# Places of the edges in source order: two column halves, one product for both halves of the base, six PSUM banks

## The chip, the cores and the metric

The kernel runs on one core of a Trainium2 chip. The metric is the device time of one execution in microseconds. The kernel before was run three times; its median is 3303.43 us.

## The reference, cut to what matters

The reference is a graph network of four blocks over 3125 nodes and 53125 edges, each edge with a source `src` and a target `dst` (sorted by `dst`) and 128 edge features. What matters here is the start, and the third block, a GIN with batch norm over the edges:

```python
for l in range(3):
    x = jnp.concatenate([h[src], e], axis=1)      # per edge
    x = x @ W1[l].T + b1[l]
    mu, var = jnp.mean(x, axis=0), jnp.var(x, axis=0)
    x = relu((x - mu) * rsqrt(var + BN_EPS) * gamma[l] + beta[l])
    h = jax.ops.segment_sum(x @ W2[l].T + b2[l], dst, num_segments=n_nodes)
    if l < 2:
        h, e = relu(h), relu(e)
```

The batch statistics need sums of `relu(e)` over the edges of each source node. Edges come sorted by target, so the kernel also writes the edge rows into DRAM a second time, ordered by the 128-node tile of their source (`by_tile`). For that each edge needs its place in this order, which is an integer worked out in the kernel: the number of edges of all lower tiles, plus those of its own tile in earlier chunks of 128 edges, plus those of its own tile in lower partitions of its own chunk.

## The kernel before, in words

Nodes lie in 25 tiles of 128 (`N_TILES`), edges in 104 groups of 4 chunks (`NG * GC` = 416 chunks), edge 128 c + p at partition p of column c. Every engine has a program of its own, written out by hand, and semaphores order them; nothing is scheduled by a planner.

The stages that matter, by the spans of the profile:

- **Setup, 0 to 37 us.** VectorE (DVE) makes `masks[:, t, :]`, for each of the 25 source tiles the 128x416 one-hot of the edges whose source is in tile t (L1277). TensorE (PE) counts them per chunk (L772), DVE scans the counts into `chunk_base`, a 25x416 table of where each chunk's edges of each tile begin, and splits it into two bf16 terms `base_hi` and `base_lo` (L1288, L1289).
- **Places, 37 to 70 us.** For each tile t PE accumulates three 128x416 products in one PSUM bank: the strictly upper triangle times the mask (L783, the number of earlier edges of that tile in the chunk), and a broadcast column of the identity times `base_hi` (L784) and times `base_lo` (L785). DVE copies the result where the mask is set (L1294, `copy_predicated`), alternately into two accumulators. Four banks are used in turn. At the end one addition of the two accumulators writes the integers `place` (L1296).
- **Counting, 70 to 350 us.** DVE, only after L1296, makes one-hots of the edges of each group (L1307) and adds the PE's products into a dense adjacency matrix in SBUF (L1318), 104 groups. PE multiplies them (L817) and, from group 21 on, does part of the first aggregation beside it (L793, L802).
- **Block 0, 350 to 546 us**: dense aggregations and two MLPs, ending in the tables `tabs` and `tabd`, one row for each node, in SBUF `tN`.
- **Block 1, from 568 us**: a pass over all edges. GpSimd (POOL) gathers rows of `tabs` from DRAM (L503); the other engines follow group by group.

Beside these, **POOL** writes the edge rows to `by_tile` with indirect DMAs (L2267, two for a pair of chunks, `put_rows`), from the moment `place` exists: pairs 0 to 127, then 128 to 187, then it goes on to block 1's gathers; the last 20 pairs follow after these. **SyncE's queue (SP)** loads the rows of each pair into a ring of four stages (`load_pairs`, L2396) and can load pair q only when pair q - 4 has been written. In SP's program the loads of pairs up to 187 stand ahead of the stores of `tabs` and `tabd` to DRAM (L2444), and POOL waits for all eight of these stores before the first gather of block 1.

```python
            put_rows(*PUT_ENDS[0:2])          # POOL; PUT_ENDS = (0, 128, 188, 208)
            ...
            load_pairs(PUT_ENDS[1] + SPILLS * STAGES, PUT_ENDS[2])    # SP: pairs 148 to 187
            ...
            for n in (1, 3, 5, 6):            # SP: stores of the tables
```

Of the kernel before, what the change touches and what calls it, by code (L numbers as in the profile page):

```python
# [51 lines left out]
PAIRS = NG * GC // 2  # L52
PUT_ENDS = (0, 128, 188, PAIRS)

# [121 lines left out]
def build(nc, x_n, x_t, e_t, e_rows, src_g, idx_g, dst_p, dst_row, src_p, weights, cols, rows, eps, gammas, out):  # L176
    with ExitStack() as ctx:
        def sb(name, shape, dt=F32):
            return ctx.enter_context(nc.sbuf_tensor(name, shape, dt))
# [9 lines left out]
        ident_h = sb("ident_h", [D, D], BF16)  # L189
# [38 lines left out]
        upper_h = sb("upper_h", [D, D], BF16)  # L228
        tile_sel = sb("tile_sel", [D, 2 * N_TILES - 1], BF16)
        tile_col = sb("tile_col", [D, 4])  # L230
# [98 lines left out]
        base_hi, base_lo = (scratch[0:N_TILES, 2048 + k * NG * GC // 2:2048 + (k + 1) * NG * GC // 2].bitcast(BF16) for k in range(2))  # L329
# [421 lines left out]
        def pe_program(pe):  # L751
# [16 lines left out]
            pe.wait_ge(S["consts"], 10)  # L768
            for t in range(N_TILES):
                if t in (0, MASKS_FIRST):  # L770
                    pe.wait_ge(S["setup_to_pe"], 5 if t else 4)
                mm = pe.matmul(cnt_ps, tile_sel[:, N_TILES - 1 - t:2 * N_TILES - 1 - t], masks[:, t, :], start=(t == 0),  # L772
                               stop=(t == N_TILES - 1))
            mm.then_inc(S["setup_to_dve"], 1)
            pe.wait_ge(S["setup_to_pe"], 6)
# [3 lines left out]
            for t in range(N_TILES):  # L779
                if t > 3:  # L780
                    pe.wait_ge(S["setup_to_pe"], 8 + t - 4)
                to, tile = psum[:, t % 4, 0:NG * GC], ident_h[0:N_TILES, t:t + 1].to_broadcast([N_TILES, D])
                pe.matmul(to, upper_h[:, :], masks[:, t, :], start=True, stop=False)  # L783
                pe.matmul(to, tile, base_hi, start=False, stop=False)  # L784
                pe.matmul(to, tile, base_lo, start=False, stop=True).then_inc(S["setup_to_dve"], 1)  # L785
# [88 lines left out]
            pe.wait_ge(S["setup_to_pe"], 33)  # L874
# [32 lines left out]
            def gin(wa, wb, fold=False):  # L907
                pe_product(pe, T.turns("a" * N_BLOCKS), [(W(wa), a0)], ("gin_in", T["gin_in"]))
                if fold:
                    pe.transpose(st_ps[:, 0:D], W("msg_2"), ident[:, :])  # L910
                    pe.transpose(st_ps[:, D:2 * D], row("msg_b2"), ident[:, :]).then_inc(S["setup_to_dve"], 1)
                if fold:
                    pe.wait_ge(S["setup_to_pe"], 35)
                    pe.matmul(st_ps[:, 2 * D:3 * D], diag[:, :], W("upd_a"), start=True, stop=True)
                    pe.matmul(st_ps[:, 3 * D:3 * D + 1], W("upd_a"), msg_col, start=True, stop=True).then_inc(S["fold_mm"], 1)
                else:
                    pe_product(pe, T.turns("a" * N_BLOCKS), [(W(wb), a0)], blocks_of=("gin_hid", T["gin_hid"]))
                    count_gin(T)
# [64 lines left out]
            pe.wait_ge(S["setup_to_pe"], 36)  # L983
            pe.matmul(x_ps[0:N_TILES, 0:2], upper[0:N_TILES, 0:N_TILES], tile_col[0:N_TILES, 0:2], start=True, stop=True
                      ).then_inc(S["setup_to_dve"], 1)
            pe.wait_ge(S["setup_to_pe"], 37)
# [196 lines left out]
        def dve_program(dve):  # L1183
# [87 lines left out]
            v.did(dve.tensor_copy(upper_h[:, :], upper[:, :]))  # L1271
            for to in place_by:
                v.did(dve.memset(to, 0.0))
# [16 lines left out]
            for t in range(N_TILES):  # L1290
                dve.wait_ge(S["setup_to_dve"], 6 + t)
                if t > 1:
                    dve.wait_ge(S["setup_to_pe"], 8 + t - 2)
                dve.copy_predicated(place_by[t % 2], masks[:, t, :].bitcast(U16), psum[:, t % 4, 0:NG * GC]).then_inc(S["setup_to_pe"], 1)  # L1294
            dve.wait_ge(S["setup_to_pe"], 7 + N_TILES)
            dve.tensor_tensor(place[:, :], place_by[0], place_by[1], ALU.add).then_inc(S["tile_tables"], 1)  # L1296
            dve.wait_ge(S["tile_tables"], 1)
# [49 lines left out]
            dve.wait_ge(S["setup_to_dve"], 31)  # L1347
# [222 lines left out]
            dve.wait_ge(S["setup_to_dve"], 32)  # L1570
# [58 lines left out]
            dve.wait_ge(S["setup_to_dve"], 33)  # L1629
# [14 lines left out]
            dve.wait_ge(S["setup_to_dve"], 34)  # L1644
# [204 lines left out]
        def act_program(act):  # L1849
# [260 lines left out]
            def two_passes(l):  # L2110
# [29 lines left out]
                act.wait_ge(S["tile_tables"], 2)  # L2140
# [99 lines left out]
        def pool_program(pool):  # L2240
# [21 lines left out]
            def put_rows(lo, hi):  # L2262
                for q in range(lo, hi):
                    k = q % STAGES
                    pool.wait_ge(S[f"from_dram{k}"], 16 * (q // STAGES + 1))
                    for c in range(2):
                        pool.indirect_dma_start(by_tile[:, :], bass.IndirectOffsetOnAxis(ap=place[:, 2 * q + c:2 * q + c + 1], axis=0),  # L2267
                                                stage[:, k, c, :], None).then_inc(S[f"put{k}"], 16)

            put_rows(*PUT_ENDS[0:2])  # L2270
# [107 lines left out]
        def sp_program(sp):  # L2378
# [122 lines left out]
            for l in range(N_LAYERS2):  # L2501
# [9 lines left out]
                sp.wait_ge(S["tile_tables"], 2)  # L2511
# [120 lines left out]
```

## Time and profile before

| what | value |
|---|---|
| three runs | 3301.45, 3303.43, 3308.19 us |
| span of the profiled execution | 3301.0 us |
| PE busy | 2649.1 us (80%) |
| DVE busy | 1984.1 us (60%) |
| ACT busy | 1271.9 us (39%) |
| POOL busy | 2154.0 us (65%) |
| mean granted TensorE clock | 0.894 |

The span runs from the first to the last instruction of the profiled execution; the time of a run holds what lies around it as well. The profile gives the span of its own execution alone, so the two are told apart here only by the median: 3303.43 less 3301.0 is 2.4 us. In the profile times are us from the start of the span; PEld is the load of a weight tile, PE the matmul; `L1294` is a line of the kernel before.

### The profile page before, as it was taken

How to read it: one execution, taken by the hardware profiler on the slowest of the kernel's cores; microseconds unless marked ns; L12 is line 12 of the kernel's file. 1: busy time of each engine (PE TensorE's matmuls, PEld its weight loads, DVE VectorE, ACT ScalarE, POOL GpSimd, SP SyncE). 2: the span in 40 equal slices, each digit the busy share in tenths (PEclk: the TensorE clock that was granted, in tenths of full speed). 3: DMA queues.
4: the chain of work that ended last, by engine and by line, in shares of the span. 5: the costliest groups of instructions: out<-in, count | busy, mean ns of one | idle time of the engine just before them, and what ended most of it. 6: DMA issues, size and time to landing. Idle time of an engine off the chain costs nothing. (4 is left out here: it accounts for less than half of the span.)

```text
span 3301.0 us, 59411 instructions
## 1 busy us (share of the span) xinstructions
PE 2649.1 (80%) x14001; PEld 1764.8 (53%) x14001; DVE 1984.1 (60%) x3553; ACT 1271.9 (39%) x3069; POOL 2154.0 (65%) x2211
## 2 busy tenths in 40 slices
PE   5689895777767878888889998667779877677998
PEld 1234443556656557777766656445556555454444
DVE  6999694544444467777779847555554655555111
ACT  4777514333333456666667622111112211112111
POOL 1777776777777767777758747777755777774000
PEclk7799998777677899999989999999989999998999
DMA  2343455755665389999949745555534555555000
GB/s 98 104 108 107 150 183 151 207 165 166 165 170 161 106 295 317 331 321 321 325 156 327 277 135 171 153 158 154 158 103 149 170 156 156 157 156 179 23 1 20
DMA packets 305072, 570.42 MB, mean 173 GB/s; under 512 B 54465, under 2 KB 140406, under 8 KB 303510
## 3 DMA queue, kind: packets, MB, share of 16 engines
q1 hardware_dynamic: 204582, 299.39, 29.3%
q0 software_dynamic: 86528, 219.09, 22.4%
q10 hardware_dynamic: 13824, 50.34, 3.8%
q8 instruction: 57, 0.93, 0.1%
q14 instruction: 81, 0.66, 0.1%
HBM read 465.21 MB, written 103.66 MB: 172 GB/s over the span
## 5 line engine op out<-in xcount | busy, mean ns | idle before, releaser
L503 POOL DMA_INDIRECT region<-tab,region x624 | 602.7, 966 | 285.4 <-issue 202.4
L1037 PE MATMUL psum<-w_all,region 128*128 128x256 f32 x2496 | 642.6, 403 | 0.7 <-ACT region L2143 0.7
L2267 POOL DMA_INDIRECT by_tile<-stage,place x416 | 408.4, 982 | 197.5 <-issue 126.7
L1037 PEld LDWEIGHTS psum<-w_all,region 128*128 128x128 f32 x2496 | 489.2, 203 | 68.2 <-issue 2.1
L587 ACT COPY region<-psum 128x256 f32<-128x256 f32 (+1 forms) x420 | 143.1, 341 | 852.6 <-PE psum L580 852.6
L580 PE MATMUL psum<-region 128*64 128x256 f32 (+1 forms) x1664 | 222.0, 391 | 193.9 <-DVE region L1797 119.5
L503 POOL DMA_INDIRECT tN<-tab,region x312 | 300.1, 962 | 95.1 <-issue 94.2
L503 POOL DMA_INDIRECT tA<-tab,region x312 | 297.8, 954 | 95.1 <-issue 94.4
L1048 PE MATMUL psum<-region 128*128 128x256 f32 x1040 | 277.1, 414 | 79.8 <-DVE region L1677 79.5
L594 PEld LDWEIGHTS psum<-fold,region 128*128 128x128 f32 x1470 | 215.1, 206 | 152.6 <-issue 152.6
L594 PE MATMUL psum<-fold,region 128*128 128x64 f32 x1470 | 276.4, 309 | 0.0
L1048 PEld LDWEIGHTS psum<-region 128*128 128x128 f32 x1040 | 204.6, 204 | 132.5 <-issue 103.4
L580 PEld LDWEIGHTS psum<-region 128*64 128x64 f32 x1664 | 114.3, 149 | 266.9 <-issue 176.4
L503 POOL DMA_INDIRECT region<-tabs,region x208 | 205.4, 988 | 72.7 <-issue 71.4
L503 POOL DMA_INDIRECT tN<-tabs,region x208 | 203.7, 979 | 63.4 <-issue 59.4
L1792 DVE TENSOR_TENSOR psum<-region,psum 128x1024 f32<-128x1024 f32 x104 | 127.8, 1229 | 192.6 <-DMA region<-tab,region 178.7
L580 PE MATMUL psum<-tN,region 128*64 128x256 f32 (+1 forms) x1040 | 135.4, 382 | 108.1 <-DVE region L527 50.1
L839 PE MATMUL psum<-region,acc 128*128 128x512 fp8e4 (+1 forms) x1050 | 208.7, 363 | 14.4 <-ACT acc L1940 10.3
L2135 ACT ACTIVATE region<-region,part 128x128 f32<-128x128 f32 x524 | 166.1, 387 | 68.2 <-PE psum L1048 61.7
L1792 DVE TENSOR_TENSOR psum<-tA,psum 128x1024 f32<-128x1024 f32 x78 | 95.9, 1229 | 146.0 <-DMA tA<-tab,region 129.3
L996 PE MATMUL psum<-w_all,region 128*128 128x128 f32 x832 | 174.4, 377 | 0.0
L2368 POOL TENSOR_TENSOR region<-node_no,dst_rel 128x256 f32<-128x256 f32 x104 | 133.4, 1283 | 58.3 <-ACT region L2177 46.2
(403 smaller groups left out, 4658.9 us busy)
## 6 DMA issues: line engine op xcount, KB each, us to landing
region<-e_t SPq DMA_DIRECT2D x416, 256.0 KB
region<-by_tile SPq DMA_DIRECT2D x131, 264.0 KB, 3.0
stage<-e_rows SPq DMA_DIRECT2D x208, 132.0 KB
pre_dram<-region ACTq DMA_DIRECT2D x48, 512.0 KB, 6.0
pre_dram<-tN ACTq DMA_DIRECT2D x48, 512.0 KB, 6.0
region<-pre_dram SPq DMA_DIRECT2D x48, 512.0 KB
tN<-pre_dram SPq DMA_DIRECT2D x48, 512.0 KB, 5.1
tA<-dst_row SPq DMA_DIRECT2D x78, 256.0 KB
```

Of the source, the lines that this page charges most:

```text
L503: pool.indirect_dma_start(ring[j][:, c, at:at + width], None, table[:, :], bass.IndirectOffsetOnAxis(ap=idx[:, c:c + 1], axis=0)).then_inc ...
L580: mm = pe.matmul(acc_ps[at:at + WIN, j % 2, 0:halves * D], oh_ring[:, j % OH_SLOTS, c, :], ring[j][:, c, 0:halves * D], start=(c < 2), sto ...
L587: act.copy(win_ring[:, slot, 0:halves * D], acc_ps[:, slot, 0:halves * D]).then_inc(S["win_out"], 1)
L594: mm = pe.matmul(turned(slot)[:, h * WIN:(h + 1) * WIN], win_ring[:, slot, h * D:(h + 1) * D], fold[:, :], start=True, stop=True)
L839: mm = pe.matmul(psum[:, b, 0:hi - lo], parts[p][:, t, :], adj[:, t, lo:hi], start=(p == 0 and t == 0), stop=(p == 2 and t == N_TILES - 1))
L996: pe.matmul(part, e_ring[:, j % E_SLOTS, edges], W("msg_e"), start=(c == 0), stop=False, skip_group_check=True)
L1037: mm = pe.matmul(banks[:, 2 * (j % 2) + c // 2, (c % 2) * 256:(c % 2) * 256 + 256], e_ring[:, j % E_SLOTS, c * D:(c + 1) * D], W(f"ee{l}") ...
L1048: mm = pe.matmul(unit_ps(m), u_both[:, m % 2, c, D:2 * D], u_both[:, m % 2, c, :], start=(c == 0), stop=(c == GC - 1))
L1792: dve.tensor_tensor(edge_ps(j), p, edge_ps(j), ALU.add).then_inc(S["pre"], 1)
L2135: r = act.activation(u_both[:, m % 2, c, D:2 * D], u_rows[:, m % U_ROWS, c, 0:D], ACT.Relu, scale=unit_mask[:, bass.ds(u * GC + c, 1)])
L2267: pool.indirect_dma_start(by_tile[:, :], bass.IndirectOffsetOnAxis(ap=place[:, 2 * q + c:2 * q + c + 1], axis=0), stage[:, k, c, :], None) ...
L2368: pool.tensor_tensor(off_ring[:, j % 2, :].rearrange("p (c n) -> p c n", c=GC), node_no[:, 0:WIN].unsqueeze(1).to_broadcast([D, GC, WIN]), ...
```

## The change

The places are worked out in two halves of 208 columns, all 25 tiles of the left half first, then all of the right (`n` = 0 to 49). The two base terms lie in one 64-row operand (hi at rows 0 to 24, lo at rows 32 to 56, zeros between), and a column of `tile_both`, which is set at rows t and 32 + t, takes both in one product. The bank ring has six places, three triangle products are issued ahead (the first three before the bases exist), and `place` is written in two halves, each with an increment of `tile_tables`. POOL starts its writes after the first and waits for the second before pair 104. All later counts of the setup semaphores are moved up by 25.

```diff
+PLACE_HALVES = (slice(0, NG * GC // 2), slice(NG * GC // 2, NG * GC))
+PLACE_SLOTS, TRIANGLES_AHEAD = 6, 3
+TOTALS_SET, BASES_SET = 5, 7
...
+            def triangle(n):
+                half, t = divmod(n, N_TILES)
+                if n >= PLACE_SLOTS:
+                    pe.wait_ge(S["setup_to_pe"], BASES_SET + n - PLACE_SLOTS + 1)
+                pe.matmul(psum[:, n % PLACE_SLOTS, 0:NG * GC // 2], upper_h[:, :], masks[:, t, PLACE_HALVES[half]],
+                          start=True, stop=False)
...
+            for n in range(TRIANGLES_AHEAD):
+                triangle(n)
...
-            for t in range(N_TILES):
-                if t > 3:
-                    pe.wait_ge(S["setup_to_pe"], 8 + t - 4)
-                to, tile = psum[:, t % 4, 0:NG * GC], ident_h[0:N_TILES, t:t + 1].to_broadcast([N_TILES, D])
-                pe.matmul(to, upper_h[:, :], masks[:, t, :], start=True, stop=False)
-                pe.matmul(to, tile, base_hi, start=False, stop=False)
-                pe.matmul(to, tile, base_lo, start=False, stop=True).then_inc(S["setup_to_dve"], 1)
+            for n in range(2 * N_TILES):
+                half, t = divmod(n, N_TILES)
+                pe.matmul(psum[:, n % PLACE_SLOTS, 0:NG * GC // 2], tile_both[0:WIN, t:t + 1].to_broadcast([WIN, D]),
+                          base_both[:, PLACE_HALVES[half]], start=False, stop=True).then_inc(S["setup_to_dve"], 1)
+                if n + TRIANGLES_AHEAD < 2 * N_TILES:
+                    triangle(n + TRIANGLES_AHEAD)
...
+            v.did(dve.tensor_tensor(tile_both[:, :], ident_h[:, 0:N_TILES], ident_h[:, 32:32 + N_TILES], ALU.add))
+            v.did(dve.memset(base_both, 0.0))
...
-            for t in range(N_TILES):
-                dve.wait_ge(S["setup_to_dve"], 6 + t)
-                if t > 1:
-                    dve.wait_ge(S["setup_to_pe"], 8 + t - 2)
-                dve.copy_predicated(place_by[t % 2], masks[:, t, :].bitcast(U16), psum[:, t % 4, 0:NG * GC]).then_inc(S["setup_to_pe"], 1)
-            dve.wait_ge(S["setup_to_pe"], 7 + N_TILES)
-            dve.tensor_tensor(place[:, :], place_by[0], place_by[1], ALU.add).then_inc(S["tile_tables"], 1)
-            dve.wait_ge(S["tile_tables"], 1)
+            for half, part in enumerate(PLACE_HALVES):
+                for t in range(N_TILES):
+                    n = half * N_TILES + t
+                    dve.wait_ge(S["setup_to_dve"], TOTALS_SET + n + 1)
+                    if n > 1:
+                        dve.wait_ge(S["setup_to_pe"], BASES_SET + n - 1)
+                    dve.copy_predicated(place_by[n % 2][:, part], masks[:, t, part].bitcast(U16),
+                                        psum[:, n % PLACE_SLOTS, 0:NG * GC // 2]).then_inc(S["setup_to_pe"], 1)
+                dve.wait_ge(S["setup_to_pe"], BASES_SET + (half + 1) * N_TILES)
+                dve.tensor_tensor(place[:, part], place_by[0][:, part], place_by[1][:, part], ALU.add).then_inc(S["tile_tables"], 1)
+            dve.wait_ge(S["tile_tables"], 2)
...
-            put_rows(*PUT_ENDS[0:2])
+            put_rows(0, PAIRS // 2)
+            pool.wait_ge(S["tile_tables"], 2)
+            put_rows(PAIRS // 2, PUT_ENDS[1])
```

The order on PE at the start of the places, before (`upper_h` is the triangle, `acc` holds the masks, `tN` the bases, `tile_sel` selects a row of the counts):

```order
L772 MATMUL psum<-acc,tile_sel 25x416 x25
L776 MATMUL psum<-tile_col,upper 25x1
L783 MATMUL psum<-acc,upper_h 128x416
L784 MATMUL psum<-tN,ident_h 128x416
L785 MATMUL psum<-tN,ident_h 128x416
L783 MATMUL psum<-acc,upper_h 128x416
L784 MATMUL psum<-tN,ident_h 128x416
L785 MATMUL psum<-tN,ident_h 128x416
```

and the same place in the changed kernel, where L778 is the triangle and L795 the product of both base terms:

```order
L784 MATMUL psum<-acc,tile_sel 25x416 x25
L778 MATMUL psum<-acc,upper_h 128x208 x3
L790 MATMUL psum<-tile_col,upper 25x1
L795 MATMUL psum<-tN,tile_both 128x208
L778 MATMUL psum<-acc,upper_h 128x208
L795 MATMUL psum<-tN,tile_both 128x208
L778 MATMUL psum<-acc,upper_h 128x208
L795 MATMUL psum<-tN,tile_both 128x208
```

Three triangles have moved ahead of the small product with `tile_col`. After that PE changes between a 64-row and a 128-row weight tile at every instruction, where before two of three in a row had 25 rows.

The order on DVE at the end of the places, before:

```order
L1294 COPY_PREDICATED tN<-acc,psum 128x416
L1294 COPY_PREDICATED acc<-acc,psum 128x416
L1296 TENSOR_TENSOR place<-acc,tN 128x416
L1307 TENSOR_SCALAR tN<-tN 128x500 x8
```

and in the changed kernel at the end of the first half (L1311 is the copy, L1314 the addition into `place`):

```order
L1311 COPY_PREDICATED tN<-acc,psum 128x208
L1311 COPY_PREDICATED acc<-acc,psum 128x208
L1314 TENSOR_TENSOR place<-acc,tN 128x208
L1311 COPY_PREDICATED tN<-acc,psum 128x208
L1311 COPY_PREDICATED acc<-acc,psum 128x208
```

The first addition, on which POOL's first write now waits, stands ahead of the second 25 copies; the one-hots of the counting (L1325 there) still stand behind all 50.

## Rows read from the trace of the kernel before

**Rows 1.** Page, part 4: the chain that ended last.

```profile
PE 3%; DVE 0%; ACT 0%; issue 0%; DVEq 0%; ACTq 0%
```

**Rows 2.** Waits (engine, line, what for: us in total, times, longest), POOL and SP.

```profile
POOL by_tile L2267 <- DVE place L1296: 67.2, 1, 67.2
SPq L2403 <- DMA by_tile<-stage,place: 401.7, 174, 56.4
```

**Rows 3.** Timeline (start us, us, engine, line, op), around the hand-over to block 1.

```profile
540.42 10.08 SPq L2396 DMA_DIRECT2D stage<-e_rows  x5
544.32 0.89 DVE L1532 TENSOR_TENSOR tN<-psum,row_all 128x512 f32<-128x512 f32 x2 [1.21 <-PE psum L690]
551.22 0.38 SPq L2444 DMA_DIRECT2D tabs<-tN  x1
556.45 3.70 SPq L2444 DMA_DIRECT2D tabs<-tN  x1
557.67 0.96 POOL L2267 DMA_INDIRECT by_tile<-stage,place  x1 [0.30 <-issue]
568.21 0.98 POOL L503 DMA_INDIRECT region<-tabs,region  x1 [9.58 <-issue]
572.30 0.69 DVE L1589 TENSOR_TENSOR region<-tA,win_node 128x512 bf16<-128x512 int32 x1 [26.22 <-DMA region<-tabd]
```

**Rows 4.** Timeline, end of the places.

```profile
67.64 0.55 PE L785 MATMUL psum<-tN,ident_h 25*128 25x416 bf16 x1
68.23 0.62 DVE L1294 COPY_PREDICATED acc<-acc,psum 128x416 f32<-128x416 uint16 x1 [0.64 <-PE psum L785]
68.88 0.59 DVE L1296 TENSOR_TENSOR place<-acc,tN 128x416 int32<-128x416 f32 x1
69.51 2.16 DVE L1307 TENSOR_SCALAR tN<-tN 128x500 bf16<-128x500 f16 x8
70.41 1.39 POOL L2267 DMA_INDIRECT by_tile<-stage,place  x1 [67.15 <-DVE place L1296]
```

**Rows 5.** Timeline, start of the places; one tile of 25.

```profile
37.02 0.35 PE L783 MATMUL psum<-acc,upper_h 128*128 128x416 bf16 x1 [1.89 <-DVE tN L1289]
39.14 0.53 PE L783 MATMUL psum<-acc,upper_h 128*128 128x416 bf16 x1
39.60 0.52 PE L784 MATMUL psum<-tN,ident_h 25*128 25x416 bf16 x1
39.92 0.55 PE L785 MATMUL psum<-tN,ident_h 25*128 25x416 bf16 x1
40.40 0.53 PE L783 MATMUL psum<-acc,upper_h 128*128 128x416 bf16 x1
```

**Rows 6.** Windows (stretch: length, busy PE, PEld, DVE, ACT, POOL, PEclk, DMA share, GB/s).

```profile
39.00:68.00 29.00, 29.00 (x70) 5.23 (x69) 14.24 (x23) 0.00 (x0) 0.00 (x0) 0.50 0.00 1
83.00:100.00 17.00, 8.90 (x20) 2.31 (x20) 15.11 (x31) 10.67 (x29) 13.11 (x13) 0.50 0.37 99
```

**Rows 7.** Groups by shape on DVE, 0 to 70 us (busy us, mean ns).

```profile
L1256 DVE TENSOR_TENSOR tN<-tN,psum 128x208 f32<-128x208 f32 x2 | 0.7, 350 | 0.0
L1273 DVE MEMSET acc<- 128x416 f32 x1 | 0.4, 405 | 0.0
```

**Rows 8.** Timeline, PE, block 1: groups of four with 128-row and 64-row weights.

```profile
598.84 0.39 PE L1000 MATMUL psum<-region 128*128 128x128 bf16 x4
599.16 0.39 PE L1003 MATMUL psum<-region 64*128 64x128 bf16 x4
599.48 0.66 PE L580 MATMUL psum<-region 128*64 128x128 f32 x8
```

**Rows 9.** Timeline, PE, counting, where part of the aggregation begins beside it.

```profile
133.88 1.82 PE L817 MATMUL psum<-tN 128*128 128x500 bf16 x4 [1.52 <-DVE tN L1307]
137.32 1.01 PE L817 MATMUL psum<-tN 128*128 128x500 bf16 x4
138.17 1.46 PE L802 MATMUL psum<-region,acc 128*128 128x512 fp8e4 x6
```

More of the change, by code:

```diff
@@ L229, in build @@
         tile_sel = sb("tile_sel", [D, 2 * N_TILES - 1], BF16)
+        tile_both = sb("tile_both", [D, N_TILES], BF16)
         tile_col = sb("tile_col", [D, 4])
@@ L328, in build @@
         chunk_base = scratch[0:N_TILES, 2560:2560 + NG * GC]
-        base_hi, base_lo = (scratch[0:N_TILES, 2048 + k * NG * GC // 2:2048 + (k + 1) * NG * GC // 2].bitcast(BF16) for k in range(2))
+        base_both = scratch[0:WIN, 2048:2048 + NG * GC // 2].bitcast(BF16)
+        base_hi, base_lo = base_both[0:N_TILES, :], base_both[32:32 + N_TILES, :]
         part2_w = part2[:, :, :].rearrange("p t f -> p (t f)").bitcast(F32)
@@ L873, in pe_program @@
             pe.transpose(x_ps[:, D:2 * D], row("ln_g"), ident[:, :])
-            pe.wait_ge(S["setup_to_pe"], 33)
+            pe.wait_ge(S["setup_to_pe"], 58)
             pe.matmul(x_ps[:, 0:1], ones[:, :], small[:, 14:15], start=True, stop=True).then_inc(S["setup_to_dve"], 1)
@@ L912, in gin @@
                 if fold:
-                    pe.wait_ge(S["setup_to_pe"], 35)
+                    pe.wait_ge(S["setup_to_pe"], 60)
                     pe.matmul(st_ps[:, 2 * D:3 * D], diag[:, :], W("upd_a"), start=True, stop=True)
@@ L982, in pe_program @@
             pe.wait_ge(S["pass_ready"], T["pass_ready"] + 1)
-            pe.wait_ge(S["setup_to_pe"], 36)
+            pe.wait_ge(S["setup_to_pe"], 61)
             pe.matmul(x_ps[0:N_TILES, 0:2], upper[0:N_TILES, 0:N_TILES], tile_col[0:N_TILES, 0:2], start=True, stop=True
                       ).then_inc(S["setup_to_dve"], 1)
-            pe.wait_ge(S["setup_to_pe"], 37)
+            pe.wait_ge(S["setup_to_pe"], 62)
             pe.matmul(x_ps[:, 0:3 * TABLE], ones[0:N_TILES, :], unit_all, start=True, stop=True).then_inc(S["setup_to_dve"], 1)
@@ L1346, in dve_program @@
             dve.tensor_scalar(small[:, 14:15], small[:, 14:15], NP - 0.5, None, ALU.is_lt).then_inc(S["setup_to_pe"], 1)
-            dve.wait_ge(S["setup_to_dve"], 31)
+            dve.wait_ge(S["setup_to_dve"], 56)
             dve.tensor_tensor(irregular[:, :], x_ps[0:1, 0:1], small[0:1, 12:13], ALU.add).then_inc(S["irregular_set"], 1)
@@ L1568, in dve_program @@
             gin(1, tA, "g2", "bt2")
-            dve.wait_ge(S["setup_to_dve"], 32)
+            dve.wait_ge(S["setup_to_dve"], 57)
             dve.tensor_copy(diag[:, :], st_ps[:, 0:D]).then_inc(S["setup_to_pe"], 1)
@@ L1628, in dve_program @@
             dve.tensor_copy(units, whole).then_inc(S["setup_to_pe"], 1)
-            dve.wait_ge(S["setup_to_dve"], 33)
+            dve.wait_ge(S["setup_to_dve"], 58)
             dve.wait_ge(v.sem, v.did(dve.tensor_copy(tile_col[tiles_, 2:4], x_ps[tiles_, 0:2])))
@@ L1643, in dve_program @@
                                      op0=ALU.subtract, op1=ALU.mult).then_inc(S["setup_to_pe"], 1)
-            dve.wait_ge(S["setup_to_dve"], 34)
+            dve.wait_ge(S["setup_to_dve"], 59)
             v.did(dve.tensor_copy(unit_i, x_ps[0:1, 0:2 * TABLE]))
@@ L2139, in two_passes @@
                 relu_e(0, 0)
-                act.wait_ge(S["tile_tables"], 2)
+                act.wait_ge(S["tile_tables"], 3)
                 unit_relu(0, 0, 0)
@@ L2510, in sp_program @@
                 sp_table(sp, T.turns("adadadadadada") if l else table_turns, tab2, 2 * D)
-                sp.wait_ge(S["tile_tables"], 2)
+                sp.wait_ge(S["tile_tables"], 3)
                 sp.wait_ge(S["idx_all"], 32)
```

## The prediction

> **What bounds the kernel now.** The chain of waits comes first and says little: it follows only the end of the program, 3% of the span [rows 1]. So I read the waits next. Two stand out for this change: POOL waits 67.2 us, once, for the addition that writes `place`, and SP's queue waits 401.7 us in 174 pieces for POOL's writes to `by_tile` [rows 2]. The timeline then tells who is last where block 1 begins [rows 3]. DVE makes the last piece of the tables at 544.32 and is done with it 0.89 later, at 545.2. SP is still loading edge rows until 550.5, one load for each pair that POOL has written, and can issue the first table store only at 551.22. POOL's last write is at 557.67 and its first gather at 568.21, after the stores have landed; DVE then has sat idle for 26.22 us. So DVE and PE have 6 us in hand there, and what sets the start of block 1 is the row of POOL's writes, which starts at 70.41 when `place` exists [rows 4]. What comes after 568 follows from this start.
>
> That makes two chains from the places stage, and the change moves them by different amounts. **Chain Y**: first half of `place`, POOL's 376 writes, SP's loads, the eight stores, block 1. **Chain X**: both halves, the counting, block 0, the tables. I work out both shifts, and then which one block 1 sees.
>
> **The cost of one step of the places.** Before, a tile takes 1.26 us (39.14 to 40.40), and PE is busy without a gap (29.00 of 29.00 us) at the lower of its two levels, 1.2 GHz (granted clock 0.50) [rows 5, 6]. DVE's copy takes 0.62 and DVE waits 0.64 before each [rows 4]. So PE is the bound. Streaming 416 columns at 1.2 GHz is 0.347 us, three times 1.04; the other 0.22 is a weight load that is not hidden. The intervals say where: 0.46 after the triangle and 0.48 before the next one, but 0.32 between the two 25-row products [rows 5]. Block 1 shows the same for the new pair of shapes: four 128-column products in 0.32 us (598.84 to 599.16, then to 599.48), where streaming at 2.4 GHz is 0.213, so 0.11 more for each change between 128-row and 64-row weights [rows 8].
>
> In the changed kernel a step of 208 columns is one triangle and one base product, and both change the weight rows: 2 x 0.173 + 0.22 = 0.57 us at the lower level. The bounds: not below the DVE, whose copy of 208 columns I put at 0.38 (0.62 less the 0.24 by which an addition falls from 0.59 at 416 to 0.35 at 208 columns; between 0.35 and 0.62) plus 0.04 to the next, so 0.42; not above 0.46 + 0.48 = 0.94, the whole old intervals [rows 4, 5, 7]. I take 0.57, because two rows at either level agree on the 0.11.
>
> The Trainium skill ("TensorE: Matmul & The Clock Gate", on LDWEIGHTS) says that the engine pulls the next weight load ahead of a running matmul when row groups don't conflict or it goes to the background buffer. By that, with all loads hidden, a step would be 0.35 on PE and 0.42 on DVE. This trace shows it hidden only between equal row counts. The same page says that keeping TensorE busy without gaps brings it to the full clock; in the 29 us here it stayed at 0.50. Both rules would give the rival of the fast step below, and I give them little weight for that reason.
>
> **Part by part.**
>
> - *Added before the masks*: the sum `tile_both` (128x25) and the zero fill (64x416 bf16). Each is smaller than the 128x416 fill of 0.405 us [rows 7], so together 0 to 0.81; I take 0.35. It delays the bases by as much: the first base product starts at 37.02 + 0.35 = 37.37 [rows 5].
> - *Three triangles ahead*: they run while DVE makes the bases, in which PE sat idle 1.89 us just before 37.02 [rows 5]. The scan of the counts on DVE takes its time anyway, and the small product with `tile_col` is not needed before it. I cost them at nothing; if that cover were gone, 3 x 0.48 = 1.4 us.
> - *Six banks*: PE waited for no copy before (it was the bound), so nothing.
> - *Chain Y*: the 25th base product starts 24 x 0.57 later, at 51.0. Its copy starts 0.42 after (before it was 0.59 for twice the columns: 67.64 to 68.23), takes 0.38, then 0.04, the half addition 0.35, and POOL needs the 0.94 that lay between the end of the old addition (69.47) and its first write [rows 4]. That is 53.1, against 70.41: **Y = 17.3 us**. POOL's second wait, before pair 104, is 208 writes later. The 376 writes ran from 70.41 to 557.67, 1.30 us each [rows 3, 4]; POOL's one long wait in it is the first [rows 2], so it moves as a whole.
> - *Chain X*: 47 steps of 0.57, then two base products without a triangle between (0.17 each): the last starts at 64.4. With 0.42, 0.38, 0.04, 0.35 and 0.04 the one-hots start at 65.6 instead of 69.51: **X = 3.9 us**. Bounds from the step: +9.9 at 0.42, and -14 at 0.94.
> - *What block 1 sees*: SP's first store could go at 551.22 - 17.3 = 533.9. The burst from there to the first gather took 17.0 us before, which gives 550.9. But now the tables are not all ready: the last is there at 545.2 - 3.9 = 541.3, 7.4 after the burst starts, while before the store of the last full piece was issued 5.2 after (556.45). From 556.45 to the first gather were 11.8 us, part of it a backlog of the earlier stores [rows 3]; the whole of it behind 541.3 would be 553.1, none of the backlog gives 550.9. I take 551.5, near the lower end, since the first stores of the burst are still landing then. The gain is 568.2 - 551.5 = **16.7 us**.
> - *The semaphore counts moved by 25* cost nothing.
>
> Against its own time, the profiled span would go from 3301.0 to 3284.3. The median of the runs is 2.4 above the span, and I carry that: 3303.4 - 16.7 = 3286.7 us.
>
> **The rivals.**
>
> *Fast step.* The loads hide, or the granted clock stays at 1.00, and DVE is the bound at 0.42 us. For it: half of PE's stream now has 128-row weights, where it was a third, so the engine's work is another one than that which stayed at 0.50. Against it: rows 5, 6 and 8. The first half is done at 49.6 with POOL's start, so Y = 20.8 and X = 9.9; the tables are there at 535.3, and the burst ends at 568.2 - 20.8 = 547.4. Time: 3282.6.
>
> *Only chain X counts.* POOL's earlier start is eaten before 551, by stops in its row of writes or because the stores wait for something else, and block 1 moves with DVE and PE: 3303.4 - 3.9 = 3299.5. For it: the writes share the DMA engines with the adjacency's spill to DRAM, and both move. Against it: SP's 401.7 us of waits for these writes, and the 26.22 us that DVE is idle [rows 2, 3].
>
> *Halved columns do not halve the step.* At 0.94 us a step, Y is 8.2 and X is -14.1; the tables come at 559.3, and with some 7 us for the last stores without a backlog the gather starts at 566.3. Time: about 3301.5, no change. Against it: rows 8, where 128 columns take 0.08.
>
> *Slower: the counting loses its clock.* With 6 aggregation products beside a group, PE needs 137.32 to 139.46, 2.1 us at the upper level, under DVE's 2.5 a group; at the lower level it would need 1.82 + 6 x 0.427 = 4.4 [rows 9], which is 1.9 us more than DVE. Before, the level rose within a group or two of the start of this work, after it had been low with PE half busy from 83 to 100 [rows 6, 9]. The changed stage ends at another time, and if the level rose late, each group would cost 1.9 us on chain X. It cancels the gain from the ninth group on (X below -13), and at 14 groups the time is about 3311. Nothing speaks for it but that the level is not set by the program.
>
> **How the numbers follow.** The forecast has a chance of 0.63, with its own range of 3284 to 3290 (step 0.5 to 0.7). The fast step has 0.17, a partial give-back between forecast and chain X 0.06, chain X alone or the unhalved step 0.10, slower 0.04. From 3279 to 3297 holds the first three. A measurement of this kernel can tell 0.2% (6.6 us) from no change, so faster means below 3296.8: 0.63 + 0.17 + 0.06 = 0.86, less 0.01 for a partial give-back that goes beyond it; same 0.11; slower 0.04.
>
> **What would show it.** In the profile after: steps of 0.57 us on PE in the places with the granted clock at 0.50 (0.42 and DVE without waits would be the fast step); POOL's first write at 53; the first one-hot at 65.6; the first table store at about 534 and the first gather at 551 to 553, with DVE's idle time before it still over 20 us. The prediction is wrong if the gather moves by less than POOL's first write does by more than 3 us, or if anything after block 1 gives the gain back.

## The result and the profile after

Against six runs of the kernel before (three new ones beside the three of the prediction; median 3305.44 us, 3298.27 to 3311.43), six of the changed kernel give a median of 3284.8 us (3281.03 to 3286.75): ratio 0.9936, 95% interval 0.9925 to 0.9947. The change is faster by 0.64%. The forecast was 3286.7 us within 3279 to 3297. The profiled span went from 3301.0 to 3279.8 us, 21.2 less; the mean granted clock is 0.895 (0.894 before). The profiled execution of the changed kernel is its fastest (3281.03 us). Below, each profile shows one execution.

**One step of the places.** Timeline of the kernel after on PE, then on DVE (start us, us, engine, line, operation, count, idle time before it and what released it; L778 is the triangle, L795 the product of both base terms, L1311 the copy):

```profile
38.18 0.26 PE L795 MATMUL psum<-tN,tile_both 64*128 64x208 bf16 x1 [1.88 <-DVE tN L1304]
38.38 0.26 PE L778 MATMUL psum<-acc,upper_h 128*128 128x208 bf16 x1
38.57 0.26 PE L795 MATMUL psum<-tN,tile_both 64*128 64x208 bf16 x1
...
40.61 0.36 PE L778 MATMUL psum<-acc,upper_h 128*128 128x208 bf16 x1
40.90 0.35 PE L795 MATMUL psum<-tN,tile_both 64*128 64x208 bf16 x1
41.19 0.36 PE L778 MATMUL psum<-acc,upper_h 128*128 128x208 bf16 x1
```

```profile
38.48 0.39 DVE L1311 COPY_PREDICATED acc<-acc,psum 128x208 f32<-128x208 uint16 x1 [0.35 <-PE psum L795]
...
40.72 0.39 DVE L1311 COPY_PREDICATED tN<-acc,psum 128x208 f32<-128x208 uint16 x1 [0.18 <-PE psum L795]
```

From 40.61 to 41.19 PE issues a triangle and a base product: 0.58 us, and over the 19 steps from the copy at 40.72 to that at 51.61 the mean is 0.573, where it was 1.26 for twice the columns [rows 5]. DVE waits 0.18 before each copy, so PE still is the bound. Timeline on PEld:

```profile
40.90 0.10 PEld L795 LDWEIGHTS psum<-tN,tile_both 64*128 64x128 bf16 x1 [0.18 <-issue]
```

The load of the weights starts at 40.90, with its own product and not during the one before. In the kernel before, the load of the second 25-row product (40.87, 0.01 after the load of the first) stands 0.31 ahead of its product (41.18), behind a weight tile of its own row count; the next 128-row load waits for its own product at 41.66.

The first steps are faster, 0.39, at the higher granted clock. Windows of the kernel after (stretch: length, busy PE, PEld, DVE, ACT, POOL, granted clock, DMA share, GB/s), to be read beside [rows 6]:

```profile
37.00:40.00 3.00, 1.82 (x9) 0.85 (x9) 2.58 (x7) 0.00 (x0) 0.00 (x0) 0.94 0.00 0
40.00:66.00 26.00, 25.11 (x89) 9.08 (x88) 18.17 (x49) 0.00 (x0) 9.79 (x10) 0.50 0.14 40
```

**The end of the two halves.** Timeline on DVE and on POOL, which answer to [rows 4]:

```profile
52.03 0.38 DVE L1314 TENSOR_TENSOR place<-acc,tN 128x208 int32<-128x208 f32 x1
...
65.37 0.38 DVE L1311 COPY_PREDICATED tN<-acc,psum 128x208 f32<-128x208 uint16 x1
65.78 0.38 DVE L1314 TENSOR_TENSOR place<-acc,tN 128x208 int32<-128x208 f32 x1
66.20 2.55 DVE L1325 TENSOR_SCALAR tN<-tN 128x500 bf16<-128x500 f16 x8
```

```profile
53.34 1.15 POOL L2285 DMA_INDIRECT by_tile<-stage,place  x1 [50.09 <-DVE place L1314]
```

POOL starts 17.1 us earlier (70.41 to 53.34), the counting 3.3 us earlier (69.51 to 66.20).

**The hand-over to block 1.** Timeline of the kernel after on SP's queue, POOL and DVE, which answer to [rows 3]:

```profile
533.39 0.38 SPq L2464 DMA_DIRECT2D tabs<-tN  x1
...
538.63 3.82 SPq L2464 DMA_DIRECT2D tabs<-tN  x1
```

```profile
539.55 0.96 POOL L2285 DMA_INDIRECT by_tile<-stage,place  x1 [0.30 <-issue]
550.41 0.98 POOL L508 DMA_INDIRECT region<-tabs,region  x1 [9.90 <-issue]
```

```profile
538.83 0.89 DVE L1550 TENSOR_TENSOR tN<-psum,row_all 128x512 f32<-128x512 f32 x2 [1.20 <-PE psum L695]
...
553.90 0.69 DVE L1607 TENSOR_TENSOR region<-tA,win_node 128x512 bf16<-128x512 int32 x1 [13.31 <-DMA region<-tabd]
```

The first table store stands 17.8 us earlier (551.22 to 533.39) and so does the first gather (568.21 to 550.41). The tables are ready only 5.5 us earlier (544.32 to 538.83 for their last piece), so DVE's idle time before block 1 halves, from 26.22 to 13.31. From the hand-over to the end the lead of matching DVE instructions over those of before goes 18.4 us (at 573), 15.7 (1150), 12.1 (1700), 14.9 (2400), 18.7 (3041), 21.2 (3301). The last 2.7 us of it arise in the last dense pass of TensorE, whose first 108 us have a granted clock of 0.98 in the profile before and 1.00 in that after. Another 3.3 us arise earlier (15.4 at 3028, 18.7 at 3045), where the granted clock is 0.50 from 3028 to 3038 in the profile before and 1.00 in the same place (3012 to 3020) of that after. Nothing in the change touches either place, and I put both rises down to the clock of these two executions. Without them this pair of profiles would end some 15 us apart, less than the 17.8 of block 1; the medians lie 20.6 us apart, and what makes up the difference stays open.

### The profile page after: what moved, and what is told of

It reads as the page before. It is cut to its first block and busy times, and to the rows that moved or that the text cites. A ratio compares the mean times of both kernels' runs of the same rounds, so it can differ in the third digit from the quotient of the medians.

```text
span 3279.8 us, 59515 instructions
## 1 busy us (share of the span) xinstructions
PE 2644.0 (81%) x14026; PEld 1768.6 (54%) x14026; DVE 1990.8 (61%) x3581; ACT 1272.0 (39%) x3069; POOL 2157.4 (66%) x2211
## 3 DMA queue, kind: packets, MB, share of 16 engines
q1 hardware_dynamic: 204582, 299.39, 29.8%
## 5 line engine op out<-in xcount | busy, mean ns | idle before, releaser
L852 PE MATMUL psum<-region,acc 128*128 128x512 fp8e4 (+1 forms) x1050 | 205.5, 359 | 10.5 <-ACT acc L1958 7.5
```

Source lines behind the costliest of these rows:

```text
L852: mm = pe.matmul(psum[:, b, 0:hi - lo], parts[p][:, t, :], adj[:, t, lo:hi], start=(p == 0 and t == 0), stop=(p == 2 and t == N_TILES - 1))
```

## The experiments

Three questions: does the row of POOL's writes set the start of block 1, or the tables; what does each part of the change give; and what are the 0.11 us of a weight load that is not hidden. Unless another kernel is named, an edit is made to the changed kernel.

### e1 to e4: four kernels on a slow chip

One set ran on a chip on which the kernel before itself takes 4269.75 us (35 runs, 4241.92 to 4293.63). What they were to show:

```diff
e1_late_pool:  -            pool.wait_ge(S["tile_tables"], 1)
               +            pool.wait_ge(S["tile_tables"], 2)
e2_before_176 (kernel before), e3_after_176:
               -PUT_ENDS = (0, 128, 188, PAIRS)
               +PUT_ENDS = (0, 128, 176, PAIRS)
e4_dve_late:    after the wait of DVE for both halves of place:
               +            for _ in range(20):
               +                dve.wait_ge(v.sem, v.did(dve.memset(low[:, :], 0.0)))
```

> The changed kernel, but POOL waits for both halves of place before its first write. Theory Y (the gain is POOL's earlier start, carried through SP's loads to the table stores): first write at about 67 us instead of 53.3, so chain Y is only 3.3 us ahead of before; first table store near 547, first gather of block 1 near 565 (550.4 in the changed kernel), time 3298 to 3301, that is 14 us of the gain gone. Theory X (the gain is the shorter places stage on PE and DVE): the one-hots start at 66.2 as in the changed kernel, time 3285.

> The kernel before, with 12 pairs fewer written ahead of block 1 (the second mark is 176 instead of 188) and 12 more after it. Theory Y: POOL and SP are free 30 us earlier, the table stores go as soon as the tables exist (last at 545.2), first gather at 552 to 556 instead of 568.2, so 12 to 16 us faster, about 3291, if the 30 us more of writes behind block 1 hide in the 41 us that POOL waits there. Rival (the start of the places, not the row of writes, is what counts): no change, 3305.

> The changed kernel with the same mark at 176. Theory Y with both chains now even (tables ready at 539.7, stores from 533.4 on): only the backlog of the stores goes, first gather at 547 to 550, 0 to 3 us faster than the changed kernel, 3282 to 3285. If chain X still had slack there (DVE idle 13 us before block 1): 10 us faster, 3275.

> The changed kernel with 20 fills (about 6 us) on DVE between the places and the counting; POOL's start is untouched. If the two chains are even since the change: tables ready at about 546 instead of 539.7, first gather 3 to 6 us later (553 to 556), time 3288 to 3291. If only chain Y counts: gather at 550.4, time 3285.

Measured: 4259.44 (ratio 0.9984, 0.9951 to 1.0016), 4277.71 (0.9998, 0.9971 to 1.0025), 4280.17 (1.0006, 0.9970 to 1.0043) and 4261.89 us (0.9965, 0.9937 to 0.9993). The intervals are as wide as the effects, and another machine is measured: none of the four tells the theories apart. The first three were run again (below); e4, with DVE made some 6 us late, was not, and its question, whether late tables hold up block 1, is answered by the halves alone, further down, where they are 11 us late.

What was not slower there can be read from the pages. The busiest DMA queue moved 204582 packets in 22.6% of 16 engines' span of 4278.4 us (e1) and in 29.3% of 3301.0 us (the kernel before on another chip): 967 us both times, so the packets themselves took no longer. Nor did the instructions of DVE: 1991.6 us busy in e1, 1990.5 in e10, which is the same kernel on the other chip. POOL's first write, too, stands at 66.81 us in e1 and at 66.72 in e10. From 70 to 350 us, though, DVE is busy for 131 us in e1 and for 255 in e10. So the lost time is waiting, from the counting on. In e1 the profile ascribes many waits, 645.5 us of ACT's for one, to `remote`, a releaser that e10's list of waits does not have; what it was stays open.

### e10: POOL waits for both halves

```diff
-            pool.wait_ge(S["tile_tables"], 1)
+            pool.wait_ge(S["tile_tables"], 2)
```

> The changed kernel, but POOL waits for both halves of the place integers before its first write. Theory (the row of POOL's writes sets the start of block 1): the second half is written at 66.2, the first write is at about 67.3 instead of 53.3, the first gather at about 565 instead of 550.4, and DVE's idle time before block 1 is again over 20 us; about 3299, ratio 0.997 to 0.999. Rival (only the chain over the counting and the tables counts): the gather stays near 551 and the time at 3285.

Measured: 3300.59 us (12 runs), the kernel before beside it 3304.20 (33 runs), ratio 0.9986 (0.9975 to 0.9998). Timeline on POOL:

```profile
66.72 1.39 POOL L2285 DMA_INDIRECT by_tile<-stage,place  x1 [63.46 <-DVE place L1314]
...
566.67 0.98 POOL L508 DMA_INDIRECT region<-tabs,region  x1 [9.53 <-issue]
```

and on DVE:

```profile
537.72 0.89 DVE L1550 TENSOR_TENSOR tN<-psum,row_all 128x512 f32<-128x512 f32 x2 [1.20 <-PE psum L695]
570.25 0.69 DVE L1607 TENSOR_TENSOR region<-tA,win_node 128x512 bf16<-128x512 int32 x1 [30.77 <-DMA region<-tabd]
```

This is the cleanest test. The 50 copies, the counting and the tables are those of the changed kernel (the tables even 1.1 us earlier than there); only POOL starts 13.4 us later. The gather comes 16.3 us later (POOL's row of writes also took 3.2 us longer, 489.4 for 486.2), and the ratio goes from 0.9936 to 0.9986, 0.5% or 16.5 us. Without POOL's earlier start nearly the whole gain is gone; the rival by which only the tables count falls.

### e7: one product for both terms, without halves

The kernel before with `tile_both` and the 64-row operand, at full width; POOL starts after the one addition.

```diff
-                pe.matmul(to, tile, base_hi, start=False, stop=False)
-                pe.matmul(to, tile, base_lo, start=False, stop=True).then_inc(S["setup_to_dve"], 1)
+                pe.matmul(to, tile, base_both[:, :], start=False, stop=True).then_inc(S["setup_to_dve"], 1)
```

> Both base terms in one product, nothing else: 25 steps of 416 columns, POOL starts after all of them. Step 2 x 0.347 + 0.22 = 0.91 us: one-hots at 62 (X = 7.5), first write at 63 (Y = 7.5), first gather near 561, time 3297 to 3299.

Measured: 3299.02 us (8 runs), ratio 0.9973 (0.9961 to 0.9985). Timeline on DVE, then on POOL:

```profile
39.74 0.62 DVE L1297 COPY_PREDICATED acc<-acc,psum 128x416 f32<-128x416 uint16 x1 [0.30 <-PE psum L786]
40.66 0.62 DVE L1297 COPY_PREDICATED tN<-acc,psum 128x416 f32<-128x416 uint16 x1 [0.30 <-PE psum L786]
...
61.26 2.16 DVE L1310 TENSOR_SCALAR tN<-tN 128x500 bf16<-128x500 f16 x8
...
566.60 0.69 DVE L1592 TENSOR_TENSOR region<-tA,win_node 128x512 bf16<-128x512 int32 x1 [30.28 <-DMA region<-tabd]
```

```profile
62.16 1.39 POOL L2270 DMA_INDIRECT by_tile<-stage,place  x1 [58.91 <-DVE place L1299]
...
563.19 0.98 POOL L505 DMA_INDIRECT region<-tabs,region  x1 [10.55 <-issue]
```

A step is 0.92 us: two streams of 416 columns (0.347 each at the lower clock) and 0.22. So the second base product had cost 0.34 with next to nothing for its weights, and both changes of the row count stay exposed. Both chains start some 8.2 us earlier, but the gather moves only by 5.0: POOL's row of writes took 489.5 us from first to last here, 487.3 before. DVE and PE, ahead by as much or more, wait it out: DVE is idle for 30.28 us, more than the 26.22 of before. An earlier counting buys nothing while POOL is last.

### e5: halves alone

Three products for each half tile, four banks, no triangle ahead; the operands are those of the kernel before, so the added fill and sum are gone too:

```diff
-PLACE_SLOTS, TRIANGLES_AHEAD = 6, 3
+PLACE_SLOTS, TRIANGLES_AHEAD = 4, 0
...
+                triangle(n)
+                pe.matmul(to, tile, base_hi[:, PLACE_HALVES[half]], start=False, stop=False)
+                pe.matmul(to, tile, base_lo[:, PLACE_HALVES[half]], start=False, stop=True).then_inc(S["setup_to_dve"], 1)
```

> Column halves and POOL's early start alone: three products for each half tile, four banks, no triangle ahead. A step is 3 x 0.173 + 0.22 = 0.74 us: first write of POOL at about 57 (Y = 13), one-hots at about 75 (X = -6), last table at 551, first gather 559 to 562, time 3296 to 3299. If the halves alone were the change: 3285.

Measured: 3293.85 us (5 runs), ratio 0.9960 (0.9946 to 0.9975). Timeline on DVE:

```profile
40.79 0.39 DVE L1306 COPY_PREDICATED acc<-acc,psum 128x208 f32<-128x208 uint16 x1 [0.35 <-PE psum L795]
41.53 0.39 DVE L1306 COPY_PREDICATED tN<-acc,psum 128x208 f32<-128x208 uint16 x1 [0.35 <-PE psum L795]
...
74.93 2.62 DVE L1320 TENSOR_SCALAR tN<-tN 128x500 bf16<-128x500 f16 x8
...
555.44 0.89 DVE L1545 TENSOR_TENSOR tN<-psum,row_all 128x512 f32<-128x512 f32 x2 [1.20 <-PE psum L694]
565.97 0.69 DVE L1602 TENSOR_TENSOR region<-tA,win_node 128x512 bf16<-128x512 int32 x1 [8.77 <-DMA region<-tabd]
```

on POOL:

```profile
542.98 1.03 POOL L2280 DMA_INDIRECT by_tile<-stage,place  x1 [0.30 <-issue]
562.68 0.98 POOL L507 DMA_INDIRECT region<-tabs,region  x1 [18.66 <-issue]
```

and on SP's queue:

```profile
551.29 0.36 SPq L2459 DMA_DIRECT2D tabs<-tN  x1
...
556.58 1.40 SPq L2459 DMA_DIRECT2D tabs<-tN  x1
```

A step is 0.74 us: the pure stream of three (3 x 0.173 = 0.52) and 0.22 for the two changes of the row count. POOL's last write is 14.7 us earlier than before (542.98 for 557.67), but the counting starts 5.4 us late (74.93), the last piece of the tables is made 11.1 us late (555.44 for 544.32), and now the other chain is last: 3.9 us lie between SP's stores, for want of DVE's pieces of the tables (551.29 to 555.16, and the last pair at 556.58), POOL idles 18.66, DVE only 8.77. The gather is 5.5 us earlier than before. So the start of block 1 is the later of two chains, and here each was last in one kernel: POOL's in the fused one, the tables' in this one. The halves alone move the gather by 5.5 us, the fused product alone by 5.0, both together by 17.8. The times do not show this: 0.40%, 0.27% and 0.64%, nearly a sum. The halves alone gained 13 us in the median where the gather of the profiled execution (3297.51 us, the second longest of the five) moved by 5.5, and beat the 3296 to 3299 that I had expected although their tables came 4 to 5 us later than expected. What makes up the difference stays open.

### e6: four banks, no triangle ahead

```diff
-PLACE_SLOTS, TRIANGLES_AHEAD = 6, 3
+PLACE_SLOTS, TRIANGLES_AHEAD = 4, 0
```

The loop issues `triangle(n)` right before the base product of n.

> The changed kernel with four banks and no triangle ahead (each triangle stands right before its base product). PE is the bound and waits for no copy, so the step stays 0.57 us; the first triangle now stands behind the bases: 0.2 to 0.6 us later. Time as the changed kernel, 3285 to 3286. If the banks mattered: a step longer than 0.57.

Measured: 3286.13 us (5 runs), ratio 0.9935 (0.9921 to 0.9949), against 0.9936 for the change. The step is the same 0.57, and the second half is written at 66.87 for 65.78. These two parts of the change are worth nothing that can be measured, as expected. Its profiled execution was the longest of the five (3296.10 us), and its gather is at 554.75 for 550.41. POOL starts 0.5 us later here (53.84), but its row of writes took 490.3 us for 486.2. Nothing in the edit touches that row, so it differs by some 4 us between executions, and so does the gather behind it.

### e8: all weights with 128 rows

Rows of zeros are added to the base operand and to its selector, so that every product has a 128-row weight tile. The result is the same number, and each product still streams 208 columns.

```diff
-        base_both = scratch[0:WIN, 2048:2048 + NG * GC // 2].bitcast(BF16)
+        base_both = scratch[:, 2048:2048 + NG * GC // 2].bitcast(BF16)
...
-                pe.matmul(..., tile_both[0:WIN, t:t + 1].to_broadcast([WIN, D]),
+                pe.matmul(..., tile_both[:, t:t + 1].to_broadcast([D, D]),
```

> The changed kernel with the base operand and its weights over all 128 rows (zeros added), so that both products have weights of one row count. If the load shows only where the row count changes, as rows 5 and 8 of before say: PE needs 0.35 us a step, DVE's copies bind at 0.39 to 0.43; first write near 50, one-hots near 60, first gather near 547.5, 3 us faster than the changed kernel, 3282. If the load shows for another reason (two products in turn, or the accumulation): step 0.57, 3285.

Measured: 3279.36 us (5 runs, 3274.10 to 3286.79), ratio 0.9914 (0.9897 to 0.9930); e6 on the same chip, with the 64-row operand, had 0.9935. Timeline on PE, then on DVE and POOL:

```profile
38.07 0.25 PE L778 MATMUL psum<-acc,upper_h 128*128 128x208 bf16 x1
38.16 0.25 PE L795 MATMUL psum<-tN,tile_both 128*128 128x208 bf16 x1
```

```profile
38.56 0.39 DVE L1311 COPY_PREDICATED tN<-acc,psum 128x208 f32<-128x208 uint16 x1
38.84 0.38 DVE L1311 COPY_PREDICATED acc<-acc,psum 128x208 f32<-128x208 uint16 x1
...
550.59 0.69 DVE L1607 TENSOR_TENSOR region<-tA,win_node 128x512 bf16<-128x512 int32 x1 [24.35 <-DMA region<-tabd]
```

```profile
47.16 1.15 POOL L2285 DMA_INDIRECT by_tile<-stage,place  x1 [43.90 <-DVE place L1314]
...
547.37 0.98 POOL L508 DMA_INDIRECT region<-tabs,region  x1 [9.86 <-issue]
```

A product follows the one before after 0.09 us, which is 208 columns at 2.4 GHz (0.087); with 64 and 128 rows in turn it took 0.19 at the same clock (38.38 to 38.57 above). The load for the product of 38.16 stands at 38.07, while the product before it runs. Timeline on PEld:

```profile
38.07 0.10 PEld L795 LDWEIGHTS psum<-tN,tile_both 128*128 128x128 bf16 x1
```

The difference of 0.10 to 0.11 us goes away when the row counts are made equal and nothing else is changed. Whether what stands in the open at a change is the load (0.10 long in the profile) or something else done at the change, the runs do not tell apart. The two halves are ready 6.2 and 12.2 us earlier than in the changed kernel, and POOL's first write at 47.16 is 3 us ahead of what was expected here. Block 1 sees 3.0 of them (550.41 to 547.37), since POOL is last again, with DVE idle for 24.35 us, and its row of writes took 489.4 us for 486.2. That the gather met the expected 547.5 is therefore luck. Against e6 it is 7.4 us earlier, and the time 0.2% or some 7 us less. The two intervals overlap, and both profiled executions are the longest of their five, so a gain in time is likely and not shown; what is shown is the step and that POOL is last.

The windows of this kernel:

```profile
40.00:45.00 5.00, 5.00 (x35) 3.35 (x33) 5.00 (x18) 0.00 (x0) 0.00 (x0) 0.74 0.00 0
45.00:50.00 5.00, 4.64 (x35) 1.86 (x34) 4.96 (x18) 0.00 (x0) 2.23 (x3) 1.00 0.06 17
```

The granted clock fell as in the changed kernel, but was back at 1.00 from 45 us on (0.74 from 40 to 45), where with 25 or 64 rows beside 128 it stayed at 0.50 to the stage's end, in the kernels before and after alike. The products also follow each other faster here, so the runs do not tell which of the two it goes by.

### e11 to e13: twelve pairs fewer ahead of block 1

The experiments so far say that POOL's writes ahead of block 1 set its start. Then fewer of them should do as much as an earlier start of them.

```diff
-PUT_ENDS = (0, 128, 188, PAIRS)
+PUT_ENDS = (0, 128, 176, PAIRS)
```

In the kernel before (e11), in the changed one (e12), and with 128-row weights (e13):

> The kernel before with 12 pairs of edge rows moved from ahead of block 1 to behind its gathers (176 for 188), so 24 of POOL's writes, 31 us, leave the chain over POOL. Theory: block 1 then waits for the tables alone, which are there at 545.2; with 6 to 11 us for the stores the first gather is at 551 to 557 instead of 568.2, and the time at 3288 to 3295, ratio 0.995 to 0.997; the 12 pairs fit into POOL's waits later. Rival (the extra writes push the later gathers, or the start of block 1 does not set the end): 3305.

> The changed kernel with the same 12 pairs moved. Theory: its start of block 1 at 550.4 is set by both chains nearly at once (tables at 539.7, the first store at 533.4), so that freeing POOL and SP by 31 us brings only the gather to 546 to 550 and the time to 3281 to 3285, ratio 0.993 to 0.994. Rival (POOL's chain alone still sets it): the gather moves well below 545 and the time to 3275 or less.

> The changed kernel with the base terms and their selector over all 128 rows (rows of zeros added) and the same 12 pairs moved. Theory: the 0.11 us for a change of the weights' row count is gone, both halves are done by 54.0, the tables are there at 525.4, and with the stores no longer behind SP's loads the first gather is at 532 to 537, 31 to 36 us ahead of the kernel before, and the time at 3268 to 3275, ratio 0.988 to 0.991. Rival (what comes before block 1 is given back later, or the extra writes push later gathers): no better than the same kernel with 188 pairs, 0.991.

Measured, each over 10 to 12 runs: 3313.76 us (ratio 1.0027, 1.0016 to 1.0037), 3310.39 (1.0011, 1.0001 to 1.0021) and 3294.19 (0.9976, 0.9965 to 0.9986). All three are slower than the same kernel with 188 pairs. The first half of my theory holds: the first gathers stand at 550.62, 546.20 and 531.68, so block 1 starts 17.6, 22.0 and 36.5 us earlier than before, at the early end of what was expected or just ahead of it. The second, that POOL's waits later would hide the moved writes, is wrong. Timeline of e11 on POOL, DVE and SP's queue, after block 1's last gather:

```profile
1172.50 0.96 POOL L2267 DMA_INDIRECT by_tile<-stage,place  x1 [0.30 <-issue]
1182.98 0.98 POOL L503 DMA_INDIRECT region<-tab,region  x1 [9.52 <-DMA tab<-tN]
```

```profile
1183.72 0.75 DVE L1677 SCALAR_TENSOR_TENSOR region<-node_no,part,region 128x512 f32<-128x512 f32 x1 [27.41 <-DMA region<-by_tile]
```

```profile
1121.85 44.21 SPq L2396 DMA_DIRECT2D stage<-e_rows  x17
...
1168.21 8.89 SPq L745 DMA_DIRECT2D tab<-tN  x4
```

and the same place in the kernel before:

```profile
1153.41 0.96 POOL L2267 DMA_INDIRECT by_tile<-stage,place  x1 [0.30 <-issue]
1163.75 0.97 POOL L503 DMA_INDIRECT region<-tab,region  x1 [9.38 <-issue]
```

```profile
1120.85 25.33 SPq L2396 DMA_DIRECT2D stage<-e_rows  x11
...
1148.29 9.50 SPq L745 DMA_DIRECT2D tab<-tN  x4
```

It is the hand-over to block 1 over again: SP loads for POOL's last writes, only then stores the next tables, and the first gather of the next pass waits for them. In the kernel before, DVE gets there hardly ahead of POOL: it starts L1677 at 1171.01 without a wait and then waits 2.29 and 4.72 us for the first two gathers. So there is little idle time in which the moved writes could hide, and each moved pair costs nearly its full two writes: DVE goes from 14.6 us ahead of the kernel before at 1150 to 14.6 behind it at 1300 in e11, 29.2 us lost, against 24 x 1.30 = 31. In e12 it is 30.7, in e13 31.0. What the move takes off ahead of block 1 ends at the tables (4.2 us in the changed kernel, 550.41 to 546.20), and what it adds behind is paid nearly in full, so it loses in all three.

## Why the prediction was right

**The step, 0.57 us.** Measured 0.573. Its two terms hold one by one: in the three kernels e5, e7 and the change the step is the stream plus 0.22, at three different streams, and e8 takes both exposed terms away by nothing but equal row counts. The Trainium skill ("TensorE: Matmul & The Clock Gate", on LDWEIGHTS) speaks of pulling a load ahead where row groups don't conflict or it goes to the background buffer; the traces agree for equal row counts (0.09 between products, the load a product ahead) and don't show it between 64 and 128 rows (0.19, each load with its own product). My bound from DVE was wrong by a third: I took 0.42 as its least interval, but in e8 the copies, 0.39 long, start 0.28 apart, the next beginning before the end of the last. It did not matter at 0.57.

**The clock.** I took 0.50 for the whole stage. The five steps from the first copy (38.48 to 40.72) took 2.24 us, not 2.85, most of them at the higher clock, which gave back 0.6; the first base product was 0.8 late (38.18 for 37.37). It stands 1.16 later than before. Of that 0.28 is the added fill and sum (the masks start at 22.44 for 22.16; I had 0.35), and 0.88 came in the count products (7.00 us for 6.12), whose time differs between executions with that same edit (6.19 in e10, 6.77 in e8). The two errors nearly cancel, which is luck: the first half was written 0.2 us after the forecast.

**Chain Y, 17.3 us.** Measured 17.1 at POOL's first write, 18.1 at its last, 17.8 at the first table store. e10 takes it away, and nearly all of the gain with it; e5 shows that it is not enough alone, since with late tables it moved the gather by 5.5 us only.

**Chain X, 3.9 us.** Measured 3.3 at the one-hots and 5.5 at the tables. Of the 0.6 us at the one-hots, 0.2 is the late first half, and another 0.2 the last two base products, which I put 0.17 apart by PE, while the copies behind them stand 0.28 apart (64.80, 65.09, 65.37). The lead shrank to 1.5 us by the end of the counting and to 0.8 at 364, and grew again in block 0. PE began the dense aggregation there 3.9 us earlier than before (398.10 for 401.97), after 1.29 us of idle time instead of 4.12, and its granted clock over that start was 0.60 before (402 to 406) and 1.00 after, another 1.6. Both belong to these two executions as far as the change tells, so the 5.5 us at the tables is not a confirmation of my 3.9. The rival in which the counting loses its clock did not happen: from 120 to 140 us it is 0.70, before 0.76, and from 140 to 350 it is 0.99, before 1.00.

**What block 1 sees, 16.7 us.** Measured 17.8. Of the difference 0.5 is chain Y, whose row of writes took 486.2 us for 487.3. The mis-sized term is the wait for the late tables: I put 0.6 us on it, it is nothing. The third store of the burst takes 3.82 us (3.70 before, 3.56 to 3.58 in e7, e8 and e10), and the tables were ready within it, at 539.7. I had held the last piece against the third pair of stores, 5.2 us into the burst; it goes with the fourth, which before stood 10.5 us into it (561.68), later than my 7.4. In e5, where the tables are late, the same term is 9.2 us (POOL ahead by 14.7, the gather by 5.5).

**DVE idle "still over 20 us"** was wrong, and by my own numbers: 26.22 - 16.7 + 3.9 is 13.4, and 13.31 was measured. A sign that fails in this way tells of a slip in the list of signs, not in the theory.

**The end.** The forecast carried the gain of block 1 to the end unchanged, 3286.7; the median is 1.9 less. That closeness is in part luck. I had taken the kernel before at 3303.43, and its six runs have 3305.44, so the gain was 20.6 us, 3.9 more than my 16.7. Of these 1.1 is at the start of block 1. The other 2.8 are within the interval of the ratio (0.11%, 3.6 us). The lead in the profiles wanders between 12 and 21 us over the later passes, in which nothing was changed, so I can't say more of them. By my own sign, that nothing after block 1 gives the gain back, the profiles are no clean yes: at 1700 us 6 of the 18 us were gone, and part of what came back was clock. The 2.4 us that I carried from span to median held more than what lies around a span, too: every execution on record with both has 1.2 to 1.6 us there.

## What to carry to other kernels

Where two chains meet at a hand-over, work out the shift of each and take the later one: the faster product alone moved the hand-over by 5.0 us, the earlier start of the slow chain alone by 5.5, and both by 17.8. Before moving work from one hand-over to a later one, look at how much idle time there is to hide it at the later one: 31 us of writes cost 29 to 31 us again. And when products with few and with all rows alternate on TensorE, try padding the small operand with rows of zeros: here it took the step from 0.57 to 0.28 us, and of the 12 us that it saved before the counting 3 to 7 reached block 1.

## What the runs showed of the hardware that I had not expected

- Each change between weight tiles of 64 and 128 rows costs 0.11 us beside the streaming, at either clock (208 columns: 0.19 us at a granted clock of 1.00, 0.29 at 0.50), and nothing (0.09 us at 1.00) when all have 128 rows.
- With 25 or 64 rows in every second or third product, 25 us and more of a nearly gapless TensorE stayed at a granted clock of 0.50 (39 to 68 us before, 40 to 66 after); with 128 rows throughout it was back at 1.00 from 45 us on, in both kernels of that kind (e8, e13).
- Predicated copies of 128x208 from PSUM last 0.39 us but start 0.28 us apart when nothing holds them up.
- One chip ran the kernel before at 1.29 times the time (4269.75 for 3305), with the same time in DMA packets and in DVE's instructions, and the same first 67 us.
- POOL's row of 376 indirect writes took between 485.7 and 490.3 us in the kernels whose row is the same.
